# Layer four's weighing with result and input of one batch stacked: 64-column matmuls, moved widenings, earlier quarters

## The reference

```
x = layernorm(x + L0(x, adj))     # per-node weights from an embedding, K = 3 powers of adj
x = layernorm(x + L1(x, adj))     # twice: relu((adj @ z) @ w[i])
x = layernorm(x + L2(x, adj))     # x @ weight_self + (adj @ x) @ weight_neighbor + bias
x = layernorm(x + L3(x, adj))     # x, adj @ x, 2 adj (adj x) - x for two equal supports, @ weight (5*64, 64)
```

## Time and profile before

| | us |
|---|---|
| median of 3 runs | 1191.92 |
| lowest, highest | 1190.46, 1192.95 |
| profiled execution | 1192.19 |
| its span | 1190.3 |
| what lies around the span | 1.9 |

### The profile page before, as it was taken

The page is one execution under the profiler, slowest core; times in us unless marked ns, Lnnn a source line. Parts: engine busy times, 40 slices in busy tenths (PEclk is TensorE's granted clock), DMA queues, the critical chain, the costliest instruction groups (busy, mean ns, idle before and its releaser), DMA issues.

```text
span 1190.3 us, 16507 instructions
## 1 busy us (share of the span) xinstructions
PE 1162.9 (98%) x5539; PEld 962.3 (81%) x5539; DVE 855.9 (72%) x1834; ACT 501.6 (42%) x681; POOL 338.3 (28%) x207
## 2 busy tenths in 40 slices
PE   9999999999999999999999999999999999999996
PEld 6788878878888788777787888887888888887885
DVE  5935899689777977789626639797847676675855
ACT  6722211102010211111127666667667766655665
POOL 0000443125411533021020304243635343240512
PEclk9999999999999999999999999999999999999998
DMA  9832123142213311110271141313543247676032
GB/s 355 353 106 63 36 71 93 58 107 72 84 49 94 102 63 41 47 60 18 65 256 71 54 124 54 124 54 95 127 107 72 44 115 166 149 182 168 27 116 74
DMA packets 183564, 122.50 MB, mean 103 GB/s; under 512 B 119024, under 2 KB 155664, under 8 KB 182192
## 3 DMA queue, kind: packets, MB, share of 16 engines
q1 hardware_dynamic: 163120, 106.68, 30.1%
q10 hardware_dynamic: 20352, 14.68, 4.2%
HBM read 81.49 MB, written 39.85 MB: 102 GB/s over the span
## 4 chain that ended last, share of the span: by engine, by line
PE 79%; DVE 9%; issue 4%; DMA 3%; SPq 2%; ACT 2%; POOL 1%; DVEq 0%; ACTq 0%; POOLq 0%
PE ps L1666 20%; PE ps L1217 17%; PE ps L1219 17%; PE ps L1571 7%; PE ps L1553 7%; PE ps L1554 7%; DVE nat L1973 2%; DVE ring L1973 2%; DMA raw<-in_at 1%; PE ps L1601 1%; PE ps L1602 1%; DVE xs L1874 1%; ACT B L1269 1%; DMA ring_g<-td 1%; SPq L2048 1%
## 5 line engine op out<-in xcount | busy, mean ns | idle before, releaser
L1217 PE MATMUL ps<-B,ops 128*128 128x512 f32 x1008 | 400.3, 397 | 5.1 <-DVE B L1273 5.1
L1219 PE MATMUL ps<-B,ops 128*128 128x512 f32 x1008 | 392.8, 390 | 0.0
L1666 PE MATMUL ps<-Tw,xs 128*128 128x512 f32 x1280 | 309.5, 392 | 4.1 <-DVE ring L1973 4.0
L1269 ACT CAST B<-pk 128x1024 fp32r<-128x1024 fp8e4 (+1 forms) x260 | 253.7, 1019 | 100.4 <-PE ps L1219 90.7
L1666 PEld LDWEIGHTS ps<-Tw,xs 128*128 128x128 f32 x1280 | 238.1, 188 | 61.6 <-DVE ring L1973 9.3
L1217 PEld LDWEIGHTS ps<-B,ops 128*128 128x128 f32 x1008 | 189.5, 188 | 47.3 <-DVE B L1273 9.8
L1219 PEld LDWEIGHTS ps<-B,ops 128*128 128x128 f32 x1008 | 189.5, 188 | 36.5
L1553 PE MATMUL ps<-B,xs 128*128 128x512 f32 x512 | 200.5, 392 | 2.3 <-DVE xs L1874 2.3
L1554 PE MATMUL ps<-B,xs 128*128 128x512 f32 x512 | 199.4, 389 | 0.0
L1973 DVE SCALAR_TENSOR_TENSOR nat<-ps,embn,nat 128x128 f32<-128x128 f32 x448 | 153.0, 341 | 38.9 <-PE ps L1666 38.3
L1973 DVE SCALAR_TENSOR_TENSOR ring<-ps,embn,ring 128x128 f32<-128x128 f32 x512 | 174.5, 341 | 0.0
(11 more groups left out here) (123 smaller groups left out, 1220.2 us busy)
## 6 DMA issues: line engine op xcount, KB each, us to landing
B<-tf ACTq DMA_DIRECT2D x24, 512.0 KB, 4.1
raw<-in_at SPq DMA_DIRECT2D x10, 1024.0 KB, 15.6
td<-raw SPq DMA_DIRECT2D x33, 256.0 KB, 2.6
raw<-in_at SPq DMA_DIRECT2D x12, 512.0 KB, 9.8
zd<-nat SPq DMA_DIRECT2D x24, 256.0 KB, 3.1
stg<-zd SPq DMA_DIRECT2D x24, 256.0 KB, 5.6
tb<-stq SPq DMA_DIRECT2D x40, 128.0 KB, 1.9
pk<-tb SPq DMA_DIRECT2D x5, 1024.0 KB, 8.3
```

Source lines behind the costliest of these rows:

```text
L1217: pe.matmul(bank, ops[:, slot, 0, m, :], of, start=not more and m == 0, stop=False, skip_group_check=more)
L1219: mm = pe.matmul(bank, ops[:, slot, 1, m, :], of, start=False, stop=m == 7, skip_group_check=more)
L1269: eng.copy(to, of).then_inc(s_exA, 1)
L1666: mm = pe.matmul(ps[:, 4 + 2 * p + q, :], src, Tw[:, wi, 512 * p:512 * p + 512], start=i == 0, stop=i == 4)
```

## The change

Weighing of layer four. The turned input of one batch and y of the same batch are stacked in one tile of 128 rows, so that one matmul with 64 weight columns does both sources for that batch. ACT copies y's rows 0 to 63 into the turn slot's rows 0 to 63 ("place", rank 2, three slots ahead of the weighing); the turned input of batch 0 is brought into the turn slot's rows 64 to 127 ("flipback", as before one slot behind the flip), that of batch 1 into the freed rows 0 to 63 of y's own slot ("beside", rank 9, three slots ahead, after the copy). `pe_beside` does 4 blocks x 2 batches, 64 columns each, no accumulation. The store of the flip becomes two DMAs (256-byte pieces). `AHEAD[4]` is 6, and three of the eight weighings in a pass stand later (`WEIGH4`; `WEIGH` is 18, 21, 24, 27, 30, 33, 36, 39). The string `EXPANDS[4]` has six V in place of five, at other places. The quarters of the last `weave` begin at step 1. The weights are laid out as four 64 x 64 blocks. Numbers of y slots (6) and turn slots (3) stay.

```diff
-    weave(3, products, 9 if fast else 22, 3, 0, None)
+    weave(3, products, 9 if fast else 22, 1 if fast else 3, 0, None)
...
-EXPANDS = {2: "AAVAAVAV" * 5, 3: "DDDAAVAAVAAVAAVADDDAAVAAVAAVAAVAAVAAVAAV", 4: "DDDAAAAAAVAAAAAVDDDAAAAAAVAAAAAVAAAAAVAA", 5: "AAAAAAAV" * 5, 6: "AAVAAVAVAAVAAVAVAAVAAVAVAAVAAVAVAAVAAVAV"}
+EXPANDS = {2: "AAVAAVAV" * 5, 3: "DDDAAVAAVAAVAAVADDDAAVAAVAAVAAVAAVAAVAAV", 4: "DDDAAAAVAAAAVAAADDDAAAAVAAAAVAAAAVAAAAVA", 5: "AAAAAAAV" * 5, 6: "AAVAAVAVAAVAAVAVAAVAAVAVAAVAAVAVAAVAAVAV"}
...
-AHEAD = {4: 7, 5: 5}
+AHEAD = {4: 6, 5: 5}
+BESIDE = 3
+WEIGH4 = [20, 22, 25, 27, 30, 33, 36, 39]
...
+            if p == 4:
+                put(w - BESIDE, 2, "place", j, p, c)
+                put(w - BESIDE, 9, "beside", j, p, c)
...
-                            mm = pe_weighed(pe, bank, c, (turn_slot2(use), W[:, w, :]), (y, W[:, w + 1, :]))
+                            if p == 4:
+                                mm = pe_beside(pe, bank, turn_slot2(use), y, W[:, 0, :])
+                            else:
+                                mm = pe_weighed(pe, bank, c, (turn_slot2(use), W[:, w, :]), (y, W[:, w + 1, :]))
...
+                    if s.kind == "place":
+                        use = "flip", j, p, c
+                        ac.wait_ge(s_y, whole_at[Step("whole", *y_of(j, p, c))])
+                        ac.wait_ge(*stored_at[use])
+                        ac.copy(turn_slot2(use)[0:C, :], y_slot2(*y_of(j, p, c))[0:C, :]).then_inc(s_keep, 1)
...
+                def batch_back(sp, to, of, q, signal):
+                    half = flat(of)[P * 256 * q:P * 256 * (q + 1)].rearrange("(a q m) -> q a m", q=C, m=32)
+                    sp.dma_start(to.rearrange("q (a m) -> q a m", m=32), half).then_inc(signal, 16)
...
+                        if s.kind == "flipped" and p == 4:
+                            to = flat(td[j, 0, c]).rearrange("(h t p x) -> h p t x", h=2, t=4, x=C)
+                            of = turn_slot2(use).rearrange("p (t h x) -> p t h x", t=4, h=2)
+                            for h in range(2):
+                                sp.dma_start(to[h], of[:, :, h, :]).then_inc(stored_at[use][0], 16)
...
+                        if p == 4:
+                            batch_back(sp, turn_slot2(use)[C:P, :], td[j, 0, c], 0, turned_at[use][0])
+                            return
...
+                    if s.kind == "beside":
+                        use = "flip", j, p, c
+                        sp.wait_ge(s_keep, keep_at[s._replace(kind="place")])
+                        batch_back(sp, y_slot2(*y_of(j, p, c))[0:C, :], td[j, 0, c], 1, turned_at[use][0])
...
+            def pe_beside(pe, bank, first, second, w):
+                for k in range(4):
+                    for q, src in enumerate((first, second)):
+                        at = k * P + q * C
+                        mm = pe.matmul(ps[:, bank, at:at + C], src[:, k * P:(k + 1) * P], w[:, q * C:q * C + C],
+                                       start=True, stop=True)
+                return mm
...
+    f2 = mats[2:4]
+    half = [w.reshape(2, 32, C).transpose(1, 0, 2).reshape(C, C) for w in f2]
-    mats += [turned[2], mats[3], turned[4], *mats[5:9], turned[6], turned[8]]
+    mats += [np.block([[f2[1], half[0]], [half[0], f2[1]]]), mats[3], turned[4], *mats[5:9], turned[6], turned[8]]
```

More of the change, by code:

```diff
@@ L507, in chunks @@
     g, p = PASSES[n]
-    for x, w in enumerate(LAST_WEIGH if n == len(PASSES) - 1 else WEIGH):
+    for x, w in enumerate(LAST_WEIGH if n == len(PASSES) - 1 else WEIGH4 if p == 4 else WEIGH):
         _, b, half = SUMS[x // 2]
@@ L1016, in second_way @@
                 unit_at = numbered(FAST, "product")
-                keep_at, raw_at = numbered(FAST, "keep"), numbered(FAST, "raw")
+                keep_at, raw_at = numbered(FAST, "keep", "place"), numbered(FAST, "raw")
                 form_at = numbered(FAST, "form", start=len(split_at))
@@ L1051, in second_way @@
                         use, i = (s.kind, s.j, s.p, s.c), TURN_SLOT[s.kind, s.j, s.p, s.c]
-                        n_slot[i] += 16
+                        n_slot[i] += 32 if (s.kind, s.p) == ("flip", 4) else 16
                         stored_at[use] = s_tw[i], n_slot[i]
                         if s.kind == "flip":
-                            n_slot[i] += 16
+                            n_slot[i] += 32 if s.p == 4 else 16
                             turned_at[use] = s_tw[i], n_slot[i]
@@ L1516, in sp_step @@
                         sp.wait_ge(s_turn, turn2_at[Step(*use)])
-                        if s.kind == "flipped":
+                        if s.kind == "flipped" and p == 4:
[3 more added lines that the diff above has]
+                                sp.dma_start(to[h], of[:, :, h, :]).then_inc(stored_at[use][0], 16)
+                        elif s.kind == "flipped":
                             to = flat(td[j, 0, c]).rearrange("(t p x) -> p t x", t=4, x=P)
```

## The result

The changed kernel takes 1198.72 us in the median of 4 runs (1198.0 to 1200.24), before beside it 1191.19: ratio 1.0054, 95% interval 1.0036 to 1.0073. It is slower by 0.5%. The forecast was 1190.8 with a range up to 1197.5: the time lies above the range, on the side of the third rival.

The account below looks back on a forecast made before the run. TensorE was taken to set the time in layer four, with weight loads bounding its weighings. Terms of -0.8, 0, +0.5, 0 and -0.8 summed to -1.1 us, giving a median of 1190.8 us, range 1185.5 to 1197.5.

Parts of the forecast that it names:

- the third rival: Transfers beside the result queue on SP behind stores awaiting DVE's flip; ten weighings late by 0.7 us, 1197.3 us; chance 0.25.
- Term 1: Layer-four weighing matmuls: weight loads set the 111 ns pair, so 64 columns save almost nothing, -0.8 us.
- The second rival: Layer-four weighings: streamed columns, not loads, bound a pair, so it halves; 1178 us; chance 0.09.
- Term 2: Widenings and new ACT copies at pass starts: gains and losses cancel, 0 us (-2.8 to +3.7).
- Term 3: Second half of the weighing's input, transferred three slots ahead: four or so late, +0.5 us (0 to +9.6).
- Term 4: Layer-four weighings moved to later slots: their results are needed only in the next pass, 0 us.
- Term 5: Last stage of layer 0, quarters begun at step 1: half of the gap near 498 us saved, -0.8 us.
- the first rival: Across the change, small gains add up and the losses don't come: 1188.0 us; chance 0.20.

Follow-up runs that it names:

- the halved load: Changed kernel with each of layer four's 64-column matmuls split into two whose stationary operand has 64 columns: 1197.08 us, a single run.
- The run alone: Kernel before, with only the quarters of the last stage of layer 0 begun at step 1: 1190.63 us, ratio 0.9993 (0.9981 to 1.0005).
- the run with the changed rank: Changed kernel with the transfer beside the result at rank 7 instead of 9, ahead of the next flip's stores on SP: 1190.7 us, ratio 0.9983.
- the run with the filler: Changed kernel with 13 extra float32 matmuls of 128 columns on PE ahead of the one late transfer near 851 us: 1195.66 us, ratio 1.0036.

## Why the prediction was wrong

*Term 1 (64 columns save nothing) was right* and explains why nothing paid for the late transfer. The loads that had run dry told it before the change was built, and the halved load shows it from the other side. The size was a little off: -0.8 was forecast, and by distances a weighing costs 0.03 to 0.04 us more than before, some +0.6 in all; why is not shown. The second rival is out. The rule of the Trainium skill that it went with (TensorE: Matmul & The Clock Gate, section "Back-to-back issue gap"), an estimated 56 ns for such a pair, doesn't hold behind a load of 128 columns: 108 ns here in the chain and 114 by distance. That page of the Trainium skill itself calls the formula the gap of an isolated matmul and says that it leaves out the load, which the prediction didn't say. The rule on loads in the same page of the Trainium skill (section "LDWEIGHTS (loading the stationary operand)") agrees: an estimated 107 ns for 128 columns, 108 here, and 53 for 64, 57 here in the order that doesn't alternate. The 57 alone can't tell the two rules apart, since both come near it; the 108 can.

*Term 2* had the right first part, 1.67 and 0.5 us gone. What the stacking does to the pass behind layer four was put at +1.2 and is +0.5. So the term was -1.7 in place of 0.

*Term 3 is the step that failed*: "I take four or so, +0.5 us". The sum for one transfer that nothing disturbs was about right (median landing 2.7 us and an issue of 0.58, against 3.0 and 0.36), and two of the three late ones cost 1.0 us together. But the +0.5 has no working: four late ones at the term's own 0.6 us are 2.4. And two things were missing. The step took its landing from the median, though the earlier trace rows has 4.2 us as the most for a turn-back and 6.5 for a store, and didn't ask what else is in flight at that slot: the ring's first three pieces of the second layer-four pass are reloads, issued by ACT just behind slot 24 of the first, where the transfer for the weighing at slot 27 stands. And it priced a late transfer by the wait alone. PE at rest for 3.2 us also lost 3.0 us by the clock. So in place of +0.5 the runs showed 6.2 us for this one transfer, and 1.0 for two others.

*The third rival* had the mechanism, with its place on SP (rank 8 ahead of rank 9, DVE's flip before both), and by the prediction's own sign, more than 3 us of waits at the weighings between 804 and 936 us, it is the one that holds (3.2 + 1.0). It was given 0.25. Its form was wrong: not ten weighings late by 0.7 us, but three of sixteen, one of them by 3.2 us and paid twice. That its 1197.3 came near 1198.7 is luck.

*Term 4* (moved weighings, 0): nothing waits for them. *Term 5*: the wait of 1.7 us near 498 is gone; waits in that stretch went from 3.0 to 2.5 us. The run alone has 0.8 in the middle of an interval that holds zero.

Two readings in the prediction are off without bearing on this: VectorE and ScalarE are busy for 44.7 to 48.9 us in the earlier trace rows, not from 42, and in the first rival two thirds of term 2 are 1.9 and all of term 5 is 1.7, where 1.6 and 1.5 stand.

With the late transfer mended the whole change stands at 1189.2 to 1190.7, where the forecast was 1190.8. That is in part luck: term 1 was 1.4 us too low, term 2 1.7 us too high, and in the run with the changed rank the small waits for transfers in layer four cost 0.5 us more than was put down.

## What to carry to other kernels

Before narrowing a matmul, look for the spacing of weight loads where the engine had run dry: if it equals the spacing of the pairs, a narrower moving operand saves nothing, and a narrower stationary one did here. For every transfer that a change moves nearer to its use, list what stands ahead of it on its queue, with what those steps wait for, and what bulk traffic is issued in the same slots; a median landing doesn't tell it. A stall of TensorE can cost nearly its length again through the clock, as the one of 3.2 us did here.

## What was not expected of the hardware

Pairs whose stationary operands have 64 columns and whose outputs alternate between the upper and the lower 64 rows come 34 ns apart in the chain (1.08 us for 32; 40 ns by distance), against 57 ns (64 by distance) in the order that doesn't alternate. And one 128 KB transfer in 128-byte pieces took 5.4 us to land among three of 512 KB on the other queue, two issued before it and one after (6.6 us in the run with the filler), and 2.7 us without them.
